# Row statistics, threshold-search steps and state scaling moved to ScalarE, in an attention and sparse-network kernel

## The reference

```python
# attention half: 16 heads of 32, chunks of C = 128 rows, a decaying state kv per head
q, k, v = x @ Wq, x @ Wk, x @ Wv          # q and k with rotary
inter  = (q_i * q_decay) @ kv
intra  = ((q_i @ k_i.T) * dmask) @ v_i
kv     = r_C * kv + (k_i * k_decay).T @ v_i
att    = rms_norm(inter + intra) @ Wo
# network half, on layernorm(x)
z      = xn @ ternary(W_syn).T + b_syn     # 2048 units
thresh = the 204th largest of z in its row
h      = relu(z) where z >= thresh, else 0
y      = layernorm(xn + h @ ternary(W_out).T + b_out)
out    = att + y
```

## Time and profile before

| | us |
|---|---|
| median of 3 timed runs (lowest, highest) | 987.61 (985.12, 988.73) |
| the profiled run's own time | 985.76 |
| its span, first to last instruction | 983.6 |
| one step in the middle of the span | 28.37 |

### The profile page before, as it was taken

How to read it: one execution, slowest core, us unless ns; L and a number is a source line. 1 busy time by engine, 2 the same in 40 slices (tenths; PEclk the granted TensorE clock), 3 DMA queues, 4 the chain that set the end, 5 groups by cost and what they waited for, 6 DMA issues and landing times.

```text
span 983.6 us, 22329 instructions
## 1 busy us (share of the span) xinstructions
PE 906.9 (92%) x8467; PEld 440.7 (45%) x8467; DVE 874.6 (89%) x2290; ACT 521.8 (53%) x654; POOL 800.9 (81%) x684
## 2 busy tenths in 40 slices
PE   5847899999999999999999999999999999999987
PEld 2423544444444444444444444444444444444434
DVE  6878899989999989999999999999999988999896
ACT  6787445555444555554455555444555554455542
POOL 1547588888988888899888888988888899888854
PEclk9968999999999999999999999999999999999979
DMA  9865535434544354343434434444354454434331
GB/s 327 259 172 97 108 68 85 98 75 88 97 77 82 70 98 87 76 97 77 97 66 87 97 72 91 93 81 82 70 98 87 76 98 78 97 64 89 75 67 43
DMA packets 257423, 94.50 MB, mean 96 GB/s; under 512 B 243488, under 2 KB 243744, under 8 KB 256544
## 3 DMA queue, kind: packets, MB, share of 16 engines
q1 hardware_dynamic: 253472, 85.64, 44.0%
q10 hardware_dynamic: 3840, 7.41, 2.1%
HBM read 24.34 MB, written 8.39 MB: 33 GB/s over the span
## 4 chain that ended last, share of the span: by engine, by line
POOL 37%; DVE 36%; issue 12%; PE 8%; DMA 4%; ACT 2%; SPq 1%; DVEq 0%; POOLq 0%; ACTq 0%
DVE area L1572 10%; POOL kvs L811 6%; DVE pair_a L1438 4%; DVE area L1371 4%; DVE Pr L1438 4%; POOL pair_b L788 4%; POOL pair_b L781 4%; POOL ahl L765 3%; POOL area L714 3%; POOL area L719 3%; PE rows L1037 3%; POOL pair_c L805 3%; POOL area L726 2%; DVE area L1365 2%; DVE pair_b L1551 2%
## 5 line engine op out<-in xcount | busy, mean ns | idle before, releaser
L971 PE MATMUL proj<-wqkv,xT 128*128 128x512 f16 x1152 | 261.6, 384 | 3.0 <-ACT area L463 2.4
L971 PE MATMUL proj<-wsynT,xT 128*128 128x512 f16 x1024 | 249.6, 388 | 4.6 <-DMA wsynT<-xrn 3.3
L971 PEld LDWEIGHTS proj<-wqkv,xT 128*128 128x128 f16 x1152 | 112.2, 99 | 137.1 <-issue 6.4
L971 PEld LDWEIGHTS proj<-wsynT,xT 128*128 128x128 f16 x1024 | 93.9, 99 | 118.4 <-issue 11.9
L760 POOL TENSOR_TENSOR hl<-area,hl 128x2048 f16<-128x2048 f32 x31 | 126.6, 4083 | 4.3 <-ACT hl L561 0.8
L1083 PE MATMUL p_ffn<-woutT,area 128*128 128x512 f16 x480 | 110.1, 380 | 0.0
L1113 PE MATMUL p_ffn<-woutT,area 128*128 128x512 f16 x480 | 108.5, 379 | 0.0
L1472 DVE MAX8 cand<-area 128x8 f32<-128x128 f32 x512 | 107.4, 275 | 1.1
L566 ACT ACTIVATE pair_b<-pair_b,c 128x512 f32<-128x512 f32 x29 | 23.6, 814 | 155.4 <-DVE c L1567 155.4
L1572 DVE SCALAR_TENSOR_TENSOR area<-area,c 128x2048 f32<-128x2048 f32 x32 | 101.1, 3161 | 1.1
L1365 DVE SCALAR_TENSOR_TENSOR area<-proj,c,gb 128x512 f32<-128x512 f32 x128 | 91.9, 738 | 8.5 <-PE proj L971 6.9
(11 more groups left out here) (236 smaller groups left out, 1805.8 us busy)
## 6 DMA issues: line engine op xcount, KB each, us to landing
xrn<-in_L_attn_x_dram SPq DMA_DIRECT2D x32, 256.0 KB, 3.2
out_dram<-pair_b SPq DMA_DIRECT2D x29, 256.0 KB, 2.1
woutT<-in_L_ffn_W_syn_dram ACTq DMA_DIRECT2D x2, 1024.0 KB, 11.1
area<-in_L_ffn_W_syn_dram ACTq DMA_DIRECT2D x2, 1024.0 KB, 11.9
woutT<-in_L_ffn_W_out_dram SPq DMA_DIRECT2D x2, 1024.0 KB, 6.7
area<-in_L_attn_Wq_dram ACTq DMA_DIRECT2D x1, 1024.0 KB, 6.9
area<-in_L_attn_Wk_dram ACTq DMA_DIRECT2D x1, 1024.0 KB, 9.7
area<-in_L_attn_Wv_dram ACTq DMA_DIRECT2D x1, 1024.0 KB, 11.8
```

What stands on the lines that cost most here:

```text
L971: last = nc.tensor.matmul(bank, xT[:, b.par, k, :], w, start=m == 0, stop=m == len(pairs) - 1)
```

## The change

The diff does the following.

- `row_stats(a)`, `row_shift(a)` (from step 2 on), `out_stats(d)` and `out_shift(d)` go from DVE to ACT. In place of bn_stats and bn_aggr ACT makes a sum over 512 columns (Copy with an accumulator), a mean, a sum of squared differences (Square with the mean as bias), and a scaled variance. The sum for the second norm comes from an accumulator output added to `network_out` on DVE. `row_stats` and `row_shift` of the prologue and of steps 0 and 1 stay on DVE.
- The five one-column instructions of the threshold search go from DVE to ACT, as `search_begun`, `guess_moved` and `guess_settled`. `diagonal(u)` now stands behind the first count and `guess_moved`.
- The scaling of the state goes from POOL (one instruction) to ACT (`state_scaled`, four instructions of 32 columns).
- On ACT `hidden_high(u)` now stands behind the second count, `guess_settled` and the first `qkv_out`. Behind `third_count` stand `qkv_out(b, 2)`, `state_scaled`, `row_stats`, `out_stats`, `row_shift`, `normalised`.
- On POOL the power for the first norm goes from ahead of `hidden_low` to behind `attention_low`, and `biases(b)` goes ahead of `low_half`.
- On DVE `probs(t, 2)` and `probs(t, 3)` go ahead of `z_chunk(b, 0)`.

```diff
+            def row_stats(a):                                  # ScalarE
+                act.wait_ge(S[f"x_loaded{a.par}"], a.half * 16 + 16)
+                nc.scalar.activation(dump_x, slot(xr, a), ACT.Copy, accum_out=xsum).then_inc(S["ln_stat"], 1)
+                wait(act, "ln_stat", a, 4, 1)
+                nc.scalar.activation(xmean, xsum, ACT.Copy, scale=-1.0 / E).then_inc(S["ln_stat"], 1)
+                wait(act, "ln_stat", a, 4, 2)
+                nc.scalar.activation(dump_x, slot(xr, a), ACT.Square, bias=xmean, accum_out=xvar).then_inc(S["ln_stat"], 1)
+                wait(act, "ln_stat", a, 4, 3)
+                nc.scalar.activation(ve, xvar, ACT.Identity, scale=1.0 / (E * XS * XS), bias=eps_x).then_inc(S["ln_stat"], 1)
+            def row_shift(a):
+                wait(act, "r256_ready", a, 1, 1)
+                nc.scalar.activation(nm, xmean, ACT.Copy, scale=r256).then_inc(S["nm_ready"], 1)
+            def out_stats(d):
+                wait(act, "y_ready", d, 1, 1)
+                nc.scalar.activation(ymean, ysum, ACT.Copy, scale=-1.0 / E).then_inc(S["yst"], 1)
+                wait(act, "yst", d, 4, 1)
+                nc.scalar.activation(dump_y, net(d), ACT.Square, bias=ymean, accum_out=yvar).then_inc(S["yst"], 1)
+                wait(act, "yst", d, 4, 2)
+                nc.scalar.activation(veD, yvar, ACT.Identity, scale=1.0 / E, bias=eps_y).then_inc(S["yst"], 1)
+            def out_shift(d):
+                wait(act, "rD_ready", d, 1, 1)
+                nc.scalar.activation(mrD, ymean, ACT.Copy, scale=rD).then_inc(S["yst"], 1)
+            def state_scaled(t):
+                wait(act, "state_ready", t, 1, 0)
...
+                for g in range(HG):
+                    head = slice(g * DH, (g + 1) * DH)
+                    nc.scalar.activation(kvs[:, head], state[:, head], ACT.Copy,
+                                         scale=rc[:, t.n % CHUNKS, g:g + 1]).then_inc(S["kvs_ready"], 1)
+            def search_begun(t):
+                wait(act, "guess_ready", t, 1, 1)
+                nc.scalar.activation(pre, nt0, ACT.Identity, bias=noff).then_inc(S["nt_step"], 1)
+            def guess_moved(t):
+                wait(act, "sum1", t, 1, 1)
+                wait(act, "nt_step", t, 5, 1)
+                nc.scalar.activation(nt1, s1, ACT.Identity, scale=ndh, bias=pre).then_inc(S["nt_step"], 1)
+            def guess_settled(t):
+                wait(act, "nt_step", t, 5, 2)
+                nc.scalar.activation(pre, nt1, ACT.Identity, bias=noff).then_inc(S["nt_step"], 1)
+                wait(act, "sum2", t, 1, 1)
+                wait(act, "nt_step", t, 5, 3)
+                nc.scalar.activation(nt2, s2, ACT.Identity, scale=ndh, bias=pre).then_inc(S["nt_step"], 1)
+                wait(act, "nt_step", t, 5, 4)
+                nc.scalar.activation(t2, nt2, ACT.Copy, scale=-1.0).then_inc(S["nt_step"], 1)
...
             def first_step():                                  # ScalarE, step 0
                 t = Tile(0, 0)
+                search_begun(t)
                 first_count(t)
+                guess_moved(t)
                 second_count(t)
+                guess_settled(t)
                 out_mean()
                 normalised(Tile(1, 0))
                 third_count(t)
+                state_scaled(t)
...
             def step(act, i, p):                               # ScalarE, steps 2 to 30
+                search_begun(t)
+                first_count(t)
+                guess_moved(t)
                 diagonal(u)
-                first_count(t)
+                second_count(t)
+                guess_settled(t)
+                qkv_out(b, 0)
                 hidden_high(u, z[:, u.par, :])
-                if t.n == 2:
-                    second_count(t)
-                qkv_out(b, 0)
-                if t.n > 2:
-                    second_count(t)
+                qkv_out(b, 1)
                 attention_high(u)
-                qkv_out(b, 1)
                 third_count(t)
+                qkv_out(b, 2)
+                state_scaled(t)
                 if a:
+                    row_stats(a)
+                out_stats(d)
+                if a:
+                    row_shift(a)
                     normalised(a)
-                qkv_out(b, 2)
-                if d:
-                    out_normalised(d)
                 attention_out(t)
+                out_shift(d)
+                out_normalised(d)
                 qk_high(b)
...
             def step(pool, i, p):                              # GpSimd
-                wait(pool, "state_ready", t, 1, 0)
-                k = rc[:, t.n % CHUNKS, :]
-                nc.gpsimd.tensor_tensor(kvs.rearrange("p (g e) -> p g e", g=HG), state.rearrange("p (g e) -> p g e", g=HG),
-                                        k.unsqueeze(2).to_broadcast([P, HG, DH]), ALU.mult).then_inc(S["kvs_ready"], 1)
...
-                if a:
-                    wait(pool, "ln_stat", a, 3, 3)
+                if a and t.n < 2:
+                    wait(pool, "ln_stat", a, 4, 4)
                     power(r256, ve, "r256_ready")
...
                     attention_low(u)
...
+                if a and t.n > 1:
+                    wait(pool, "ln_stat", a, 4, 4)
+                    power(r256, ve, "r256_ready")
+                if t.n > 1:
+                    biases(b)
...
             def step(dve, i, p):                               # VectorE, steps 2 to 30
-                if a:
-                    row_stats(a)
-                search_begun(t)
-                first_step(t)
-                if a:
-                    row_shift(a)
-                if d:
-                    network_out(d)
-                    out_stats(d)
+                network_out(d)
                 attention_normalised(u)
-                if d:
-                    out_moments(d)
-                second_step(t)
                 below(t)
                 segments(t, 0)
                 segments(t, 1)
                 q_decayed(t)
                 probs(t, 0)
                 probs(t, 1)
-                z_chunk(b, 0)
                 probs(t, 2)
                 probs(t, 3)
-                if d:
-                    out_shift(d)
+                z_chunk(b, 0)
                 segments(t, 2)
...
             def network_out(d):
+                wait(dve, "yst", d, 4, 0)
+                nc.vector.scalar_tensor_tensor(net(d), p_ffn, so, slot(xn, d), ALU.mult, ALU.add,
+                                               accum_out=ysum).then_inc(S["y_ready"], 1)
```

More of the change, by code:

```diff
@@ L655, in last_steps @@
                 third_count(T31)
+                out_stats(T29)
                 attention_out(T31)
+                out_shift(T29)
                 diagonal(T31)
@@ L661, in last_steps @@
                 out_normalised(T29)
+                out_stats(T30)
                 last_high(2)
                 last_high(3)
+                out_shift(T30)
                 out_normalised(T30)
@@ L767, in out_root @@
             def out_root(d):
-                wait(pool, "yst", d, 4, 3)
+                if d.n == NT - 1:
+                    pool.wait_ge(S["half_stat"], 4)
+                else:
+                    wait(pool, "yst", d, 4, 3)
                 nc.gpsimd.tensor_tensor(rD, veD, mhalf, ALU.pow).then_inc(S["rD_ready"], 1)
@@ L845, in step @@
                 if t.n > 1:
-                    biases(b)
                     rotary(b)
@@ L865, in last_steps @@
                 hidden_low(T30, z[:, 0, :])
+                out_root(T29)
                 squares_added(T31)
@@ L1401, in prologue @@
                 then(nc.vector.tensor_scalar(ndh, pc[:, 55:56], -0.5 / 359.4, None, ALU.mult))
-                then(nc.vector.tensor_scalar(off, pc[:, 55:56], 0.5 / 359.4 * (N - 2 * (TOPK - AIM)), None, ALU.mult))
+                then(nc.vector.tensor_scalar(noff, pc[:, 55:56], -0.5 / 359.4 * (N - 2 * (TOPK - AIM)), None, ALU.mult))
                 then(nc.vector.tensor_scalar(pc[:, 56:57], pc[:, 50:51], -1.0, None, ALU.mult))
@@ L1525, in hidden @@
                                                ALU.mult).then_inc(S["h_ready"], 1)
-            def first_step(t):
-                wait(dve, "sum1", t, 1, 1)
-                wait(dve, "nt_step", t, 5, 1)
-                nc.vector.tensor_scalar(nt1, s1, ndh, pre, ALU.mult, ALU.add).then_inc(S["nt_step"], 1)
-            def second_step(t):
-                wait(dve, "nt_step", t, 5, 2)
-                nc.vector.tensor_scalar(pre, nt1, off, None, ALU.subtract).then_inc(S["nt_step"], 1)
-                wait(dve, "sum2", t, 1, 1)
-                wait(dve, "nt_step", t, 5, 3)
-                nc.vector.tensor_scalar(nt2, s2, ndh, pre, ALU.mult, ALU.add).then_inc(S["nt_step"], 1)
-                wait(dve, "nt_step", t, 5, 4)
-                nc.vector.tensor_scalar(t2, nt2, -1.0, None, ALU.mult).then_inc(S["nt_step"], 1)
             def network_out(d):
@@ L1728, in last_steps @@
                 hidden(T30, z[:, 0, :])
-                search_begun(T31)
```

(7 more changed lines are left out.)

73 lines of the change are left out of this document (35 added, 38 removed).

## The result

The changed kernel takes 972.65 us (four runs, 972.07 to 973.72), the kernel before took 987.1 beside it (985.12 to 988.73): ratio 0.986, interval 0.984 to 0.988. It is faster by 1.4%, or 14.4 us. The forecast was 988.5, the range 973 to 1005, so the time is just outside the range, on the side of rival A (974 at 27.9 us a step). The profiled run took 972.45, its span is 970.7 against 983.6.

What follows compares the result with a forecast made beforehand. No engine alone but a ring of waits was taken as the bound; the new ring is 23.5 + 4.9 = 28.4 us against 28.37. 29 steps by +0.03 (+0.9) and edges +1.8 on 985.76 gave 988.5 us, range 973 to 1005.

Steps and rivals of the forecast that it cites:

- rival A: ACT's leg is shorter and PE becomes the bound: faster, 974 us at 27.9 a step, 959.5 at the floor; chance 0.27.
- a ring with PE's floor behind it: A middle step is a cycle of waits between engines, 28.37 us, 0.97 above PE's busy time of 27.40.
- the first ring: DVE's row_shift waits for POOL's power, then below, POOL, and probs 0.97 us late for PE; the change empties it.
- The walk from the guess: Sum over ACT, then POOL, from the guess to the end of the squares: 23.5 us in the new ring.
- That is 4.1 behind the squares.: Squares to the next guess's start, 4.1 us; inside POOL's first qk_low subtraction, so the guess ends at 4.9.
- rival A in its second form: The guess slips ahead of POOL's subtraction, needing 0.35 us, and 1 us goes; PE then bounds; rival's chance 0.27.
- Edges: "+1.5 (0 to 3).": Steps 0 and 1: DVE's ternary weights and step 1's diagonal and hidden_high come later, costing 1.5 us.
- Rival B: ACT's list is the bound, with dearer small instructions and waits: slower, 28.9 us a step, 1003 us; chance 0.33.
- Rival C: Taking the scaling off POOL frees nothing because q_joined inherits the stop; part of the forecast, costs no time.
- The z chunk: Moving z_chunk(b, 0) behind the last probs on DVE is worth nothing, as both orders end before PE asks.
- The rule on SBUF contention: A two-SBUF-input VectorE instruction contends with GpSimd's reads: step 28.4 us by it, 27.8 with the guess free of the stop.
- run 983: Whole kernel's forecast time in us by the skill's ScalarE prices, ACT's small instructions 0.2 us cheaper, 28.2 a step.

Runs made afterwards that it cites:

- e_step1_search_on_dve: Against the kernel after: in step 1 alone, the five one-column search instructions back on DVE, ACT in the order of before; 979.11 us.
- k: Against the kernel after: state scaling of tiles 2 and up back on POOL, ahead of q_joined; 954.10 us.
- hw: Against the kernel after: ACT's row statistics moved ahead of the third count and out_stats behind normalised, nothing moved between engines; 953.88 us.
- s: Against the kernel after: search instructions of tiles 2 to 30 back on DVE, ACT's counts and high halves in the order of before; 1005.56 us.
- r: Against the kernel after: first norm's row statistics and row_shift back on DVE ahead of network_out, POOL's power ahead of hidden_low; 992.62 us.
- o2: Against the kernel after: second norm's statistics back on DVE for tiles 2 and up, its shift behind the last segments; 980.90 us.
- g_guess_one_input: Against the kernel after: the guess on DVE as a one-input instruction, everything else the same; 967.53 us.
- ghw_order_and_guess: Against the kernel after: row statistics ahead of the third count, out_stats behind normalised, and the guess as a one-input instruction; 952.37 us.

## Why the prediction was wrong

- **What bounds.** The view of a ring with PE's floor behind it held, and so did the end of the first ring: PE no longer waits for `probs`. Of before's ring I had read DVE's side only. That `below` and `hidden_low` collided there, at 0.8 us on DVE and a stand of 2.29 on POOL, I did not say; in my walk it did not appear because `below` comes early enough there, which is so behind a stopped guess and not quite behind a free one (0.6 us on `hidden_low`).
- **The walk from the guess.** In the step from 511.16 to 539.35, nt1, the counts, `hidden_high` (forecast 8.31 behind the guess, measured 8.19), the row variance (14.8, 14.5) and `low_half` (17.8, 17.67) held. Squares ended 23.27 behind instead of 23.5. The wait ahead of the power (0.69), PE's 0.59 ahead of `squares_summed`, `below` at 6.0 and ACT's busy 20.4 are as forecast; DVE's idle time before `flags` was 1.27, not 2. One sum in it is off by 0.1: 8.31 with the copy, `attention_high`, the third count and the copy behind it (0.48, 0.52, 1.98, 0.48) makes 11.77, not 11.67. `hidden_high` ended 0.12 sooner than 8.31, which made up for it.
- **The step that failed: "That is 4.1 behind the squares."** From there the prediction lets the guess start inside POOL's subtraction and end at 4.9. It is 4.08 in four of the 27 steps (squares to 534.43, guess from 538.51), but 3.75 in most: the idle time of DVE ahead of `threshold` is 0.67 in the four, and 0.34 in the others. I had taken it from the one step of the earlier trace rows and made POOL's subtraction stop every guess. At 3.75 the start falls on the subtraction's own start, so only 10 of the 27 guesses are stopped. Stopped steps have 28.20 instead of 28.4, free ones 27.87. That is rival A in its second form ("the guess slips ahead of POOL's subtraction (it needs 0.35)"). It did not reach PE's floor, because ACT's list up to `normalised`, entered through PE's projections, has 27.87; neither I nor the rival had seen that ring. 0.41 a step less than before, times 27, is 11.0 us. Against the forecast of 28.4 the free guesses are 17/27 of 0.33, 0.21 a step; the rest, 0.2, is that even a stopped step has 28.20, since `low_half` starts at 17.67 and not at 17.9.
- **Edges: "+1.5 (0 to 3)."** The sign was wrong: -4.3 ahead of the guess of step 2, of which e_step1_search_on_dve takes back 3.1, and +2.6 between the guesses of steps 2 and 4. Of the latter, the first step took 31.66 instead of 28.04: `hidden_low` starts 8.57 behind the guess instead of 4.65, and PE stands 1.96 for POOL's squares. The second took 28.46 instead of 29.49, where PE had stood 1.77 for `probs`. I have not taken it apart further; k and hw, whose steps 0 and 1 are those of after, have 57.9 there instead of 60.1, so it is not the work moved in steps 0 and 1 alone.
- **Rival B** had the right place, ACT's list, but not the prices (0.34 and 0.10 for one operand and a gap). Those of the forecast (0.30, 0.38, 0.19) were right within 0.02: one operand took 0.28 to 0.30, two 0.39, none 0.19 to 0.20. The list is the bound of the kernel after, but at 27.87 to 28.20 a step, under the 28.37 of before and not over it.
- **Rival C** held: scaling off POOL frees nothing there. What I had not drawn from it is that on ACT, ahead of `normalised`, it costs 18.5 us.
- **The z chunk** was worth nothing, as forecast.
- **The rule on SBUF contention** (the Trainium skill, "SBUF — State Buffer", "Who interferes with whom") agrees with this: in place of the two-input guess, which took up to 1.17 us, the one-input one took 0.21. What decides is which instruction began first, and that no clause of my sum had. The other (the Trainium skill, "ScalarE: Activation LUTs", "Rules for kernel authors"), on adds and multiplies on ACT, made the run 983 by the prices that the page gives under "What ACT_TABLE_LOAD costs", and the trace's are about as cheap (0.20, 0.29 and 0.39 by operands). No run here tests its advice by itself: the search went back to DVE only together with ACT's order, and the scalings never went to DVE.

What the change did: the search on ACT, with the second count ahead of `hidden_high`, took `below` out of `hidden_low`, all but the last 0.76 us of it behind a free guess (s: 33 us worse without both). The norms' statistics off the stretch ahead of `below` kept it so (r: 20, o2: 8). The scalings gave 18.5 us of that away; hw got as much back by moving out_stats instead. These differences do not add up, as each is against the rest of the change. Not tried: any one part on the kernel before, so how the gain of 14.4 us divides over the parts stays open.

## What to carry to other kernels

Look at what POOL does when a two-input instruction on DVE starts, and not only at that instruction's own time: here moving it by a microsecond changed the time of both. Where others wait for one instruction in an engine's list, as for `normalised` here, what stands ahead of it costs: first put behind it what can stand there, and only then think of moving work to another engine. And a start that a forecast puts within 0.4 us of a stop has both outcomes: price both.

## What the runs showed of the hardware

- Of a two-input DVE instruction and a POOL one, the one that began first was the one not held: 0.01 us decided between 0.16 and 1.17 for the guess. `hidden_low` took 4.08 alone or first. It took 4.70, 4.96, 5.97 or 6.00 when `below` still had 0.76, 1.0, 2.0 or 2.1 us to go. When POOL was first, its following instruction stood until `below` was through (2.29).
- A DVE instruction of one column with one tensor input in the place of that guess took 0.21 or 0.22 in all steps (g_guess_one_input, ghw_order_and_guess).
- One-column instructions on ACT that wait for the one ahead started 0.02 to 0.1 us behind its end; an accumulator's read took 0.18 to 0.20.
- DVE's idle time ahead of `threshold`, where it reads the count of failures back and branches on it, was 0.34 or 0.67 us for the same code in the 27 steps of after (0.6 to 1.0 in most of before).
